# When the gathers are issued, and who copies what, in a deep-and-cross recommendation kernel

## The reference, cut to what matters

```
e = stack([tbl_0[ids[:, 0]], ..., tbl_38[ids[:, 38]]], axis=1)      # 512 x 39 x 16
X0 = Xi = e;  res = []
for W, b in ((W0, b0), (W1, b1), (W2, b2)):                          # 128 outputs each
    Xi = einsum('hjk,bjd,bkd->bhd', W.reshape(H, 39, Fi), X0, Xi) + b[None, :, None]
    res.append(Xi.sum(axis=2))
h = concatenate([concatenate(res, axis=1), dense_ctx], axis=1)       # 512 x 400
h = maximum(h @ W_top1 + b_top1, 0.0)
h = maximum(h @ W_top2 + b_top2, 0.0)
y = h @ W_top3
```

## Time and profile before

| | |
|---|---|
| median of three runs | 677.99 us |
| the profiled execution | 682.74 us, of which its span 680.5 us |
| PE busy | 654.7 us (96%) |
| ACT busy | 572.2 us (84%) |
| DVE busy | 518.0 us (76%) |
| POOL busy | 460.1 us (68%), in quads 2 to 12 about four fifths |
| TensorE clock granted | 0.992 on average |

### The profile page before, as it was taken

The page is one execution under the profiler, slowest core; times in us unless marked ns, Lnnn a source line. Parts: engine busy times, 40 slices in busy tenths (PEclk is TensorE's granted clock), DMA queues, the critical chain, the costliest instruction groups (busy, mean ns, idle before and its releaser), DMA issues. The chain is left out here.

```text
span 680.5 us, 10678 instructions
## 1 busy us (share of the span) xinstructions
PE 654.7 (96%) x2692; PEld 480.2 (71%) x2692; DVE 518.0 (76%) x1017; ACT 572.2 (84%) x2013; POOL 460.1 (68%) x453
## 2 busy tenths in 40 slices
PE   3699999999999999999999999999999999999998
PEld 3566776677777777777777677767777777776673
DVE  5458796787878879697878778777868787888880
ACT  2467897889898989899999889888988899899772
POOL 6468779877787878787887888777878656333000
PEclk9789999999999999999999999999999999999999
DMA  7203143323342516142331313131313221204400
GB/s 212 57 14 101 8 104 68 74 54 89 92 118 35 175 15 189 15 137 44 110 70 37 83 20 99 16 103 16 97 12 95 24 71 41 89 1 134 176 0 0
DMA packets 111121, 49.22 MB, mean 72 GB/s; under 512 B 82907, under 2 KB 94903, under 8 KB 111060
## 3 DMA queue, kind: packets, MB, share of 16 engines
q1 hardware_dynamic: 104830, 45.94, 25.6%
q0 software_dynamic: 5376, 1.45, 2.2%
q10 hardware_dynamic: 854, 1.16, 0.7%
HBM read 13.81 MB, written 5.24 MB: 28 GB/s over the span
## 5 line engine op out<-in xcount | busy, mean ns | idle before, releaser
L740 ACT ACTIVATE prod<-ps_y,xt 128x128 f32<-128x128 f32 x1792 | 492.8, 428 | 63.4 <-PE ps_y L1193 57.4
L1191 PE MATMUL ps_y<-w_hi,x_hi 128*128 128x512 f32 (+1 forms) x640 | 304.0, 475 | 7.6 <-DVE x_lo L928 3.3
L1193 PE MATMUL ps_y<-w_hi,x_lo 128*128 128x512 f32 (+1 forms) x640 | 249.2, 389 | 0.0
L1192 PE MATMUL ps_y<-w_lo,x_hi 128*128 128x512 f32 (+1 forms) x640 | 249.2, 389 | 0.0
L531 POOL TENSOR_TENSOR prod<-prod 128x512 f32<-128x512 f32 x120 | 155.1, 1292 | 90.7 <-ACT prod L740 85.6
L964 DVE SCALAR_TENSOR_TENSOR prod<-ps_y,xt,prod 128x128 f32<-128x128 f32 x576 | 163.5, 342 | 38.0 <-PE ps_y L1193 37.6
L495 POOL DMA_INDIRECT rows<-in_table,index x160 | 153.9, 962 | 47.0 <-issue 32.4
L1191 PEld LDWEIGHTS ps_y<-w_hi,x_hi 128*128 128x128 f32 x640 | 120.3, 188 | 63.7 <-issue 21.3
L972 DVE TENSOR_REDUCE prod<-prod 128x128 f32<-128x1536 f32 (+1 forms) x64 | 116.3, 1818 | 51.8 <-ACT prod L740 42.7
L1192 PEld LDWEIGHTS ps_y<-w_lo,x_hi 128*128 128x128 f32 x640 | 120.9, 189 | 43.4 <-issue 20.9
L1193 PEld LDWEIGHTS ps_y<-w_hi,x_lo 128*128 128x128 f32 x640 | 120.5, 188 | 26.0
(11 more groups left out here) (149 smaller groups left out, 378.8 us busy)
## 6 DMA issues: line engine op xcount, KB each, us to landing
room<-room SPq DMA_DIRECT2D x75, 234.0 KB
room<-room SPq DMA_DIRECT2D x45, 78.0 KB
emb_room<-rows SPq DMA_DIRECT2D x168, 5.0 KB
rows<-in_table,index POOLq DMA_INDIRECT x160
w_hi_dram<-g_all SPq DMA_DIRECT2D x5, 512.0 KB
w_lo_dram<-g_all SPq DMA_DIRECT2D x5, 512.0 KB
g_all<-in_L_rec_W SPq DMA_DIRECT2D x9, 256.0 KB
g_all<-in_L_rec_W SPq DMA_DIRECT2D x4, 512.0 KB, 3.8
```

The costliest lines, as they stand in the source:

```text
L740: ins = nc.scalar.activation(prod[:, SLOT[k] + m // 2, :, m % 2], ps_y[:, g % YBANKS, m * H:(m + 1) * H], ACT.Copy, scale=xt[:, q % 2, ti, ...
L1191: nc.tensor.matmul(y, hi, w1_hi[:, cols], start=True, stop=False)
L1192: nc.tensor.matmul(y, hi, w1_lo[:, cols], start=False, stop=False)
L1193: nc.tensor.matmul(y, lo, w1_hi[:, cols], start=False, stop=True).then_inc(y_made, 1)
```

## The change

Six edits. They all move work; the one operation that changes its kind is that POOL, not ACT and DVE, splits the dense inputs.

1. Quad 1's gathers 2 to 9 get later waits (`first_x0`, `first_z`, `first_x1_lo`, then `y_made` 1, 3, 5 and, behind the first addition of tile 0, 6 and 7).
2. ACT copies its half of quad 1's rows behind group 9 of tile 0, not behind group 3; the turning and keeping of quad 1 move from tile 0, group 7, to tile 1, group 1.
3. Quad 2's rows are turned after group 0 and kept after group 1 of tile 4, where it was 1 and 3.
4. Gathers of quads 5 to 15: one behind each of the first five additions of a quad, two behind each of the next two, one at the end, where it was 0, 2, 0, 2, 0, 4, 1, 1.
5. The split of the dense inputs is done by POOL behind the additions of tiles 61 and 62.
6. After tile 63 three banks of the perceptron's first layer, and the dense part of the fourth, stand ahead of the last sum over d, where it was two; two of the four matmuls with layer 1's known sum move ahead of layer 2's sum.

```diff
-GATHERED_IN = {(0, 1): range(0, 2), (1, 1): range(2, 4), (2, 1): range(4, 8), (3, 0): range(8, 9),
-               (3, 1): range(9, GATHERS)}
+GATHERED_IN = {(0, 0): [0], (0, 1): [1], (1, 0): [2], (1, 1): [3], (2, 0): [4], (2, 1): [5, 6], (3, 0): [7, 8], (3, 1): [9]}
-SECOND_REGROUPED_AFTER = 3
-NEXT_TURNED_AFTER, NEXT_KEPT_AFTER = [(0, 7), (0, 1)], [(0, 7), (0, 3)]
+SECOND_REGROUPED_AFTER = (0, 9)
+NEXT_TURNED_AFTER, NEXT_KEPT_AFTER = [(1, 1), (0, 0)], [(1, 1), (0, 1)]
...
-            pool.wait_ge(regrouped_dve, 1)
+            pool.wait_ge(first_x0, 1)
             gather(1, 2)
-            pool.wait_ge(emb_made, 1)
+            pool.wait_ge(first_z, 2)
             gather(1, 3)
-            pool.wait_ge(first_x0, 1)
+            pool.wait_ge(first_x1_lo, 1)
             gather(1, 4)
...
+            for g in range(5, 8):
+                pool.wait_ge(y_made, 2 * g - 9)
+                gather(1, g)
 
             add_groups(0, 0)
+            for g in range(8, GATHERS):
+                pool.wait_ge(y_made, g - 2)
+                gather(1, g)
             pool.wait_ge(pool_step, 1)
...
+                if T == TILES - 3:
+                    pool.wait_ge(late_mlp, 16 * 6)
+                    pool.wait_ge(z_used, CHUNKS * QUADS)
+                    nc.gpsimd.tensor_copy(dense_stack[0:C, :], dense_t[:]).then_inc(dense_hi_made, 1)
+                    nc.gpsimd.tensor_copy(dense_w_stack[0:C, :], wt1[0:C, K1 // P, :]).then_inc(dense_hi_made, 1)
...
-            for m in range(2):
-                known_mlp1(m, (3, 0))
-            sum_d(TILES - 1)
-            for part in (3, 0):
-                for m in range(2, MC1):
-                    known_mlp1(m, (part,))
-            pe.wait_ge(g_kept, TILES)
+            for m in range(MC1 - 1):
+                known_mlp1(m, (3, 0))
+            known_mlp1(MC1 - 1, (3,))
+            sum_d(TILES - 1)
+            known_mlp1(MC1 - 1, (0,))
+            pe.wait_ge(g_kept, TILES)
+
+            for m in range(2):
+                known_mlp1(m, (1,))
```

More of the change, by code:

```diff
@@ L545, in _ @@
             gather(1, 1)
-            pool.wait_ge(regrouped_dve, 1)
+            pool.wait_ge(first_x0, 1)
             gather(1, 2)
-            pool.wait_ge(emb_made, 1)
+            pool.wait_ge(first_z, 2)
             gather(1, 3)
-            pool.wait_ge(first_x0, 1)
+            pool.wait_ge(first_x1_lo, 1)
             gather(1, 4)
-            pool.wait_ge(first_xa, 1)
-            gather(1, 5)
-            pool.wait_ge(first_z, 2)
-            gather(1, 6)
-            pool.wait_ge(first_z, 4)
-            gather(1, 7)
-            pool.wait_ge(first_summed, 1)
-            gather(1, 8)
-            pool.wait_ge(first_x1_lo, 1)
-            gather(1, 9)
+            for g in range(5, 8):
+                pool.wait_ge(y_made, 2 * g - 9)
+                gather(1, g)
             add_groups(0, 0)
+            for g in range(8, GATHERS):
+                pool.wait_ge(y_made, g - 2)
+                gather(1, g)
             pool.wait_ge(pool_step, 1)
@@ L642, in _ @@
                     between(T // QT, T % QT, part)
+                if T == TILES - 3:
[3 more added lines that the diff above has]
+                    nc.gpsimd.tensor_copy(dense_w_stack[0:C, :], wt1[0:C, K1 // P, :]).then_inc(dense_hi_made, 1)
+                if T == TILES - 2:
+                    pool.wait_ge(dense_hi_made, 2)
+                    nc.gpsimd.tensor_tensor(dense_low, dense_t[:], dense_stack[0:C, :].bitcast(F32),
+                                            ALU.subtract).then_inc(dense_lo_made, 1)
+                    nc.gpsimd.tensor_tensor(dense_w_low, wt1[0:C, K1 // P, :], dense_w_stack[0:C, :].bitcast(F32),
+                                            ALU.subtract).then_inc(dense_lo_made, 1)
         @block.scalar
@@ L769, in _ @@
                         keep_rest_x1()
-                    if (T, g) == (0, SECOND_REGROUPED_AFTER):
+                    if (T, g) == SECOND_REGROUPED_AFTER:
                         act.wait_ge(gathered[1], 16 * GATHERS)
@@ L778, in _ @@
                         keep_x0(q + 2)
-                    if (T, g) == (TILES - 3, 4):
-                        act.wait_ge(late_mlp, 16 * 6)
-                        act.wait_ge(z_used, CHUNKS * QUADS)
-                        nc.scalar.copy(dense_stack[0:C, :], dense_t[:]).then_inc(dense_hi_made, 1)
-                        nc.scalar.copy(dense_w_stack[0:C, :], wt1[0:C, K1 // P, :]).then_inc(dense_hi_made, 1)
                     if g == 7 and T > 0:
@@ L1032, in _ @@
                                             w2_home(False, n), ALU.subtract).then_inc(w2_lo_made, 1)
-                if T == TILES - 3:
-                    dve.wait_ge(dense_hi_made, 2)
-                    nc.vector.tensor_tensor(dense_low, dense_t[:], dense_stack[0:C, :].bitcast(F32),
-                                            ALU.subtract).then_inc(dense_lo_made, 1)
-                    nc.vector.tensor_tensor(dense_w_low, wt1[0:C, K1 // P, :], dense_w_stack[0:C, :].bitcast(F32),
-                                            ALU.subtract).then_inc(dense_lo_made, 1)
                 if T == TILES - QT:
@@ L1264, in _ @@
                 nc.tensor.matmul(ps_r3, w_hi, g_lo[j % RING], start=False, stop=j == F - 1).then_inc(g_used, 1)
-            for m in range(MC1):
+            for m in range(2, MC1):
                 known_mlp1(m, (1,))
```

## The result

The changed kernel takes 689.97 us (median of four, 688.73 to 691.41), the kernel before beside it 678.35 us: ratio 1.0172, 95% interval 1.0146 to 1.0198. Forecast were 691 us and slower. A second comparison gave 689.94 against 678.68 us, 1.0147 (1.0099 to 1.0194). So the change costs 11 to 12 us by the medians, and both intervals lie clear of no change.

What follows compares the result with a forecast made beforehand. PE was taken to bound the kernel, with an ACT, POOL and `reduce_early` loop close behind. Terms 9.5 - 1.0 + 6.5 - 1.0 - 0.9 = +13.1 us on the median 677.99 gave 691 us, range 683 to 698.

Steps and rivals of the forecast that it cites:

- Two signs that the prediction named: Start: tile 0's second addition before 50 makes the first term wrong; a loss under 6 us fails the whole forecast.
- rival B: Front: spaced gathers no longer hold up ACT's signal, -3.4 and -1.5, steady gathers hidden; 680.7 us, chance 0.10.
- `x0` of quad 1: Tile 1: kept behind ACT's groups 0 and 1, done at 59.0 instead of 49.25, 9.75 us later, delaying the windows.
- PE's group 3 of tile 1 needs that bank, so it goes from 51.77 to 57.1: 5.3 us: Start: PE's first wait, for the bank of DVE's group 8 behind the late `reduce_early`, 5.3 us.
- idle for that whole time: Start: PE idles for all of the +9.5 us in three waits: group 3 of tile 1, chunk 0, chunk 2.
- the addition behind `repeat_rows(1)`: Start: tile 0's second addition on POOL, held by ACT's copies and the repeating, ends at 54.35 and delays `reduce_early`.
- One more tile like it makes 1.2 a quad: Steady part: lateness left uncovered by PE's room after tiles 47 and 48, plus one more tile, costs 1.2 us a quad.
- The room: Steady part: slack between DVE's group 8 and PE's group 3, 0.30 us in tile 47, 1.35 a tile later.
- My 8: Steady part, edit 4: 0.6 us a quad for six quads plus 0.9 for five, about 8 us.
- the shading: Steady part: about 8 lowered to +6.5 us for what the four gathers in a row cost before.
- Rival A: Steady part hides its gathers, leaving +7.6 us: 685.6 us, chance 0.22.
- rival C: Both upper ends and the slow clock's 1.5: 10 + 9 + 1.5 - 2, +18.5 or so, 696.5 us, chance 0.11.

Runs made afterwards that it cites:

- b_new_steady: The kernel before with only the gathers of quads 5 to 15 in their new places (edit 4 alone): 684.78 us, ratio 1.0084.
- a_add_ahead: The changed kernel with POOL's second addition of tile 0 ahead of its copies and repeating of quad 1's rows: 681.29 against 669.36 us for the kernel before.
- a_window_first: a_add_ahead with three of quad 2's seven gathers moved behind POOL's first multiplication of quad 1: 690.87 against 678.68 us for the kernel before.
- b_again: The kernel before, unchanged, run again for a second trace: 678.91 against 677.93 us, ratio 1.0005.
- b_behind: The kernel before with gathers of quads 5 to 15 behind the second additions, none between two additions: 668.86 against 669.36 us, ratio 0.9991.
- b_two_in_3: As b_behind, but with gathers 7 and 8 between the additions of each quad's fourth tile: 681.12 against 678.68 us for the kernel before, ratio 1.004.

## Why the prediction was right

**The sum.** From the table, old against new:

```
                                        forecast   measured
tiles 0 to 4, edits 1 and 2               +9.5      +9.2   (-0.4 in tile 0, +9.6 in tiles 1 to 3)
tiles 4 to 8, edit 3                      -1.0      -1.3
tiles 8 to 60, edit 4                     +6.5      +6.3   (means of six and of five traces)
tiles 60 to 63, edit 5                    -1.0      -0.6
behind tile 63, edit 6                    -0.9      -0.8
sum                                      +13.1     +12.8
```

The medians differ by 11.6 and 11.3. What is left, 1.2 to 1.5, is of the size of what lies ahead of tile 0: it starts at 33.53 instead of 34.87 in the first two traces. The steady term is a mean; it is 4.6 by the first two traces alone, 5.6 in the set of b_new_steady and 7.5 in that of a_add_ahead, the more the fewer wandering waits the old kernel has.

Two signs that the prediction named came out close to their limits, because the front ran faster than it had reckoned. Tile 0's second addition started at 50.08, with 50 as the limit, and tile 4 at 86.32, 6.4 us later and not 9.5, with 6 as the limit. Tile 0 started 1.3 us sooner and took 1.9 less than in the first trace. So the spans of the first two traces differ by only 8.2 us, and it takes the medians and the means of the table to see the 13 us of the forecast less what the front gives back.

**The front, rival B.** In the sets where the kernel before takes 678 us, ACT was let go 0.3 to 3.8 us behind PE's first sum in all six traces with quad 1's old gathers, and 0.1 to 0.2 in all four with the new ones; tile 0 starts at 34.4 us in the mean there, and at 32.1 in these (33.1 without a_window_first, whose 28.95 stands alone). The stretch from ACT's copies of quad 0's rows to tile 0, in which the moved gathers were issued, is 12.5 to 13.1 us in the six and 9.0 to 11.7 in the four. In b_again:

```profile
30.59 2.45 PE L1159 MATMUL ps_x<-room,w0t 128*128 128x128 f32 x14
...
34.41 0.37 ACT L715 ACTIVATE x_hi<-ps_x,columns 128x128 fp32r<-128x128 f32 x1 [6.21 <-PE ps_x L1159]
```

and in the changed kernel, whose ACT starts 0.11 behind the end of the sum:

```profile
30.03 2.58 PE L1155 MATMUL ps_x<-room,w0t 128*128 128x128 f32 x14
...
32.72 0.37 ACT L722 ACTIVATE x_hi<-ps_x,columns 128x128 fp32r<-128x128 f32 x1 [5.08 <-PE ps_x L1155]
```

So a part of rival B's gain was there, 1 to 2 us of its 4.9, and I had given it a tenth. Its own condition, tile 0 below 31.5, was not met (33.53). But in the other set b_behind, with the same old gathers, shows no lateness:

```profile
23.15 2.02 PE L1158 MATMUL ps_x<-room,w0t 128*128 128x128 f32 x14
...
25.38 0.37 ACT L714 ACTIVATE x_hi<-ps_x,columns 128x128 fp32r<-128x128 f32 x1 [3.16 <-PE ps_x L1158]
```

The gathers alone are not the cause, then; they seem to matter only where something else has made the front slow. The 8 us between the sets lie ahead of tile 0, and a good part of them ahead of any gather that edit 1 moves. ACT copies quad 0's rows at 17.4 to 18.0 us in the set at 669.36 us and at 18.6 to 22.3 in the other traces, in the first trace 4.9 us later than in b_behind; by then at most gathers 0 and 1 of quad 1 are issued. In that first trace ACT had waited long while it prepared weights, for a signal whose sender the profile doesn't name ("remote"):

```profile
17.86 0.58 ACT L688 COPY w0t<-ps_y 128x512 f32<-128x512 f32 x1 [3.68 <-remote]
...
22.33 1.84 ACT L347 COPY emb_room<-rows 32x40 f32<-32x40 f32 x8
```

In b_behind that wait is 0.99, put down to PE, and the copies wait for nothing but the rows:

```profile
17.40 1.84 ACT L346 COPY emb_room<-rows 32x40 f32<-32x40 f32 x8 [1.19 <-DMA rows<-in_table,index]
```

Why these waits are longer stays open. The sets ran on different chips, so a difference between the chips is the obvious candidate, but chip and time changed together, and no run separates them. A late signal also costs in tile 0: behind the two longest (3.5 and 3.8 us) tile 0 took 14.8 and 16.0 us instead of 13.3, at the half clock of the earlier trace rows. I had left the front's gain out of the sum, and it is of the size of what the sum has too much.

**The start, right in size and half wrong in its chain.** `x0` of quad 1 was to be 9.75 later and was 9.9, and chunk 2 follows it by the same amount. But the step "PE's group 3 of tile 1 needs that bank, so it goes from 51.77 to 57.1: 5.3 us" failed. PE waited 2.11 us before, for the turned rows, a wait that I did not have at all, and then only 2.41. Nor was PE "idle for that whole time": it waited 7.0 us and spent the other 2.6 on slower matmuls. And the addition behind `repeat_rows(1)`, which I made the head of the chain, gave back only 1.7 of the 9.6 us when it was moved (a_add_ahead), with 2.4 us of half clock in that trace's way, which I had left out of the sum. By the traces the rest hangs on the rows themselves: POOL repeats them 3.1 us behind tile 1's start instead of 5.6 ahead of it, its index and its seven gathers of quad 2 come behind that, and the windows behind both. Three late things lay side by side, and the sum came out because each alone is nearly as late. That last step is read from the order of the rows; no run brought quad 1's rows forward and left the rest.

**The steady part.** "One more tile like it makes 1.2 a quad" is close: quads 8 to 12 lose 1.1 a quad, 11 and 12 of them 1.2, against b_behind by their three waits. But the 1.2 does not follow from the working ahead of it, which ends at 0.85 behind the second tile (1.05 by the starts). The room was under-read as well: the first matmul of group 3 is recorded at 490.29 while the sum ahead of it lasts to 490.85, and only 0.44 of the wait of 0.74 was a loss. One gather alone takes 1.11 us from addition to addition in the earlier trace rows, where I had 1.20. Net of what the old places cost there themselves (181.6 us in the mean of six traces, 185.7 in that of the five new ones) it is 0.8 a quad, against my 0.9; tiles 8 to 32 lose 1.9 in all, where 0.6 a quad had made 3.6, and I had shaded the sum down from 8 to 6.5. My 8 was too much in the first quads, and the shading, which had another reason, took it back: that part is luck. That the cost needs a gather between the two additions, and that gathers behind the second are free, is shown by b_behind and b_two_in_3. Rival A (hidden) is excluded. So is rival C, 696.5 us: neither upper end was reached, and the slow clock of tile 1 added nothing.

**The end.** The split gave 0.6, not 1.0: ACT's two copies seem to have been only in part on the path, which no run separates. The half-microsecond more that the first trace of before showed behind tile 63 was of that execution.

## What to carry to other kernels

Work that is issued between two links of a loop costs what it exceeds the slack there by, while the same work behind the last link was free here: look for the 0.3 to 0.6 us of room and not for the engine's mean of 68%. When a late step is to be priced, list everything that waits for the same event, and take one away on the chip before naming one of them the cause; here three chains were late together, and removing the one I had named gave back a sixth. A slow clock costs nothing while another wait ends behind it, and its full price once that wait is gone, so it can eat the gain of a repair. Price in stretches: most columns of the table agree to 0.3 us within a group where whole times scatter by 5.

## What the runs showed of the hardware that I had not expected

The same kernel took 677.93, 669.36 and 678.68 us in the three sets, on three chips, and nearly the whole difference lies ahead of the first tile (26.2 to 26.7 us against 29 to 35); the steady quads are alike but for single waits. Those, of 0.7 to 1.5 us ahead of a quad's first group, move between tiles from one execution of a kernel to the next. And a PE that had been busy for 1.5 of 6 us then ran for over 4 us at a granted clock of 0.50, in tile 1 of the changed kernel; where the wait had moved to the end of that tile (busy for 0.3 of 3 us), the half clock moved behind it and cost 2.4 us.
